# Norm of the QKV input: sums of squares spread over all partitions by two products with ones, for blocks two to eight

## Chip, cores and metric

The kernel runs on one core of a Trainium2 chip. The metric is the device time of one execution in microseconds (us). The core has five engines that work side by side and wait for each other through semaphores: TensorE (PE, with its weight loads shown as PEld), VectorE (DVE), ScalarE (ACT), GpSimd (POOL) and SyncE (SP, which here only issues DMAs).

## The reference

`x` is 2 x 2048 x 576 (batch, tokens, channels), with 16 heads of 36 channels. What bears on the change is the first RMS norm and the QKV product:

```python
def rmsnorm(x, g, d):
    n = jnp.linalg.norm(x, axis=-1, keepdims=True)
    return x / jnp.maximum(n, EPS) * d ** 0.5 * g          # EPS = 1e-12
mod = silu(c) @ ada_w.T + ada_b                             # six parts: shift, scale, gate, twice
h = rmsnorm(x, g1, D) * (1.0 + scale_msa) + shift_msa
qkv = h @ qkv_w.T + qkv_b                                   # 576 -> 1728
q = rmsnorm(q, qg, HEAD_DIM);  k = rmsnorm(k, kg, HEAD_DIM) # per head
# then attention, projection, gated residual, a second norm, a gelu MLP of 2304, gated residual
```

All of it is in float32. The kernel feeds TensorE with values split into a high and a low part (type fp32r), so that three products stand for one.

## The kernel before

The program has a QKV stage (up to about 437 us of the span) and a main stage (attention, projection, MLP). The change lies in the QKV stage alone.

**Tiling.** Channels lie on partitions: 576 are four chunks of 128 and one of 64 (`KC` = 5 chunks). Tokens are cut into eight blocks of 512 (`BLK`), numbered i = 0 to 7, alternating between the two batch rows (r = i % 2). Each block has four tiles of 128 tokens (`TPB` = 4, t = 0 to 3). Only the first iteration and the last (of `NIT` = 4, two blocks each) are written out; those between are a hardware loop with the same body.

**One tile on TensorE** (`tile`, L787 on). The 1728 output columns stand in four PSUM banks of 432 columns, in two halves h = 0, 1. One half is 28 products of 128x432 (L798). A half may start when VectorE has emptied the same banks of the tile before. After the second half come nine transposes of the q and k of the tile before (`turn`, L753), which must wait for VectorE's `scale` (L597) of that tile. TensorE executes in order, so whatever stands behind a waiting transpose waits too.

**One tile on VectorE** (`body`, L681 on), in this order: `evac` of half 0 (L612 and L614, adding the bias); `scale` of the tile before (L590, L592, L594, L597); `evac` of half 1; the sums over heads of the squares that ScalarE has made meanwhile (L703, behind ACT L444); two, one or no `dot` products for the later modulation (L659); the low part of the transposed tile before (L603).

**The norm of the next block** runs beside the tiles of the current one. POOL sums the squared chunks into `sq_hi` and `sq_lo` (128 partitions x 512 tokens); the sum over the partitions is left. In tile t = 1, after half 0, TensorE runs `sum_squares`: for each group of 128 tokens two products with the squares as weights and two columns of ones moving (L737, L738), so that the sums stand one token to a partition, as 128x8, in `RT`. VectorE bounds them from below (L392, right after `evac` half 0), ScalarE takes the root (L366), VectorE the reciprocal (L397, right after `scale`, ahead of `evac` half 1), and after half 1 TensorE's `spread_norm` (L745, four float32 products of 128x128, each shown as two instructions) brings the result back to all partitions as 128x512 in PSUM, `RB`. At t = 2, ahead of `evac` half 0, VectorE multiplies the whole block with it (L406, 128x2560, reading `RB`); ScalarE applies the modulation (L369) and makes the high part (L386), POOL the low one.

Block 0's norm is made in the same way before the first tile, and keeps its form.

Of the kernel before, what the change touches and what calls it, by code (L numbers as in the profile page):

```python
# [10 lines left out]
ACT = mybir.ActivationFunctionType  # L11
ALU = mybir.AluOpType
AX = mybir.AxisListType

P = 128
# [5 lines left out]
KC = KF + 1  # L21
DP = KC * P
BLK = 512
# [13 lines left out]
EPS = 1e-12  # L37
# [7 lines left out]
def wait(eng, sem, value):  # L45

    if isinstance(value, int) and value <= 0:
        return
    eng.wait_ge(sem, value)
# [108 lines left out]
def qkv_phase(nc, ctx, sb, ps, first_unit, xT, cT, ada, adan, adab, wqkv, qkvb, pb, f1b, f2b, gains, qk_hi, qk_lo, v_s, m_s,  # L158
# [5 lines left out]
    st = ctx  # L164

    def sem(name):
        return ctx.enter_context(nc.semaphore("a_" + name))

    xb = sb(st, "xb", [P, 2, KC, BLK])
    tmp = sb(st, "tmp", [P, KC, BLK])  # L170
# [16 lines left out]
    rs = sb(st, "rs", [P, TPB, 2])  # L187
    sq_hi = sb(st, "sq_hi", [P, BLK], F32R)
    sq_lo = sb(st, "sq_lo", [P, BLK], F32R)
# [3 lines left out]
    w_raw2 = sb(st, "w_raw2", [P, KC, PIECE])  # L193
    w_raw3 = sb(st, "w_raw3", [P, KC, PIECE])
    root_gain = sb(st, "root_gain", [P, 1])

    awp = aw[:, 1].rearrange("p (k c) -> p k c", k=KC)
    aws, awn = (aw[:, j, 0:KC * D].rearrange("p (m c) -> p m c", m=KC) for j in range(2))
# [23 lines left out]
    sq_done, sqsum, sqhi_done, sqlo_done = sem("sq_done"), sem("sqsum"), sem("sqhi_done"), sem("sqlo_done")  # L222
    ss_done, nrm_done, rb_mm = sem("ss_done"), sem("nrm_done"), sem("rb_mm")
    r_max, r_done, xr_done = sem("r_max"), sem("r_done"), sem("xr_done")
# [11 lines left out]
    RB, MOD1 = ps[:, 4, :], ps[:, 5, 0:KC * B].rearrange("p (m b) -> p m b", b=B)  # L236
# [127 lines left out]
    def norm_act(act, i):  # L364
        act.wait_ge(r_max, i + 1)
        act.activation(rs[:], rs[:], ACT.Sqrt).then_inc(nrm_done, 1)  # L366

    def affine(act, r, m):
        act.activation(tmp[:, m], tmp[:, m], ACT.Identity, bias=mod[:, SHIFT_MSA, m, r:r + 1],  # L369
                       scale=mod[:, SCALE_MSA, m, r:r + 1]).then_inc(aff_done, 1)  # L370

    def prep_act(act, i, r, part):

        if part == 0:
            act.wait_ge(x_ld[r], 16 * (i // B + 1) if isinstance(i, int) else 8 * (i - r) + 16)
            act.wait_ge(hlo_done, KC * i)
            act.activation(tmp[:], xb[:, r], ACT.Square).then_inc(sq_done, 1)
        elif part == 1:
            norm_act(act, i)
        elif part == 2:  # L380
            act.wait_ge(xr_done, i + 1)
            for m in range(KC):
                affine(act, r, m)
            act.wait_ge(aff_done, KC * (i + 1))
            wait(act, qkv_mm, 2 * TPB * (i - 1))
            act.activation(h_hi[:, r], tmp[:], ACT.Copy).then_inc(hhi_done, 1)  # L386

    def bounded(dve, i):

        dve.wait_ge(ss_done, i + 1)  # L390
        wait(dve, rb_mm, i)
        dve.tensor_scalar(rs[:], RT, EPS * EPS, None, ALU.max).then_inc(r_max, 1)  # L392

    def reciprocal(dve, i):

        dve.wait_ge(nrm_done, i + 1)
        dve.reciprocal(rs[:], rs[:]).then_inc(r_done, 1)  # L397

    def prep_dve(dve, i, r, part):
        if part == 0:  # L400
            bounded(dve, i)
        elif part == 1:
            reciprocal(dve, i)
        else:
            dve.wait_ge(rb_mm, i + 1)
            dve.tensor_tensor(tmp[:], xb[:, r], RB.unsqueeze(1).to_broadcast([P, KC, BLK]),  # L406
                              ALU.mult).then_inc(xr_done, 1)

    HQ = slice(0, H), slice(H, QKG)

# [80 lines left out]
    def dve_part(dve):  # L491
# [22 lines left out]
        def w_low(q, half, done):  # L514

            dve.wait_ge(whi_done, q + 1)
            ks, cols = W_HALVES[half], slice(q * PIECE, (q + 1) * PIECE)
            dve.tensor_tensor(w_lo[:, ks, cols], raw[q][:, ks], f32(w_hi[:, ks, cols]), ALU.subtract).then_inc(done, 1)
# [38 lines left out]
        dve.wait_ge(mod_done, 1)  # L557
        dve.tensor_scalar(mod[:, SCALE_MSA], mod[:, SCALE_MSA], root_gain[:, 0:1], None, ALU.mult).then_inc(mod_done, 1)
        w_low(0, 0, wlo_done)
        bounded(dve, 0)  # L560
        reciprocal(dve, 0)
        w_low(0, 1, wlo_done)
        dve.wait_ge(mod_done, 2)
        dve.wait_ge(modn_add, 1)
# [113 lines left out]
        def body(it, first, last):  # L678
            for r in range(B):
                i = B * it + r  # L680
                more = not (last and r == 1)  # L681
                for t in range(TPB):
                    tt, early = TPB * i + t, first and r == 0 and t < 2
                    if last and r == 1 and t == TPB - 1:
                        last_half(0)
                        scale(tt - 1, t + 1)
                        last_scale(0)
                        turned_low(tt - 1)
                        last_half(1)
                        last_scale(1)  # L690
                        continue
                    if more and t == 2:
                        prep_dve(dve, i + 1, 1 - r, 2)
                    evac(tt, i, t, 0, early)
                    if more and t == 1:
                        prep_dve(dve, i + 1, 1 - r, 0)
                    if not (first and r == 0 and t == 0):
                        scale(tt - 1, t + 1)
                    if more and t == 1:
                        prep_dve(dve, i + 1, 1 - r, 1)  # L700
                    evac(tt, i, t, 1, early)
                    dve.wait_ge(sqt_done, tt + 1)
                    dve.tensor_reduce(ssb[:], sqb.rearrange("p (g d) -> p g d", d=HD), AX.X,  # L703
                                      ALU.add).then_inc(red_done, 1)
                    if first and r == 0 and t == 0:
                        for m in range(2, KC):
                            shift(1, m, prod)
                    for m in (DOTS_FIRST if first and r == 0 else DOTS if more else DOTS_LAST)[t]:
                        dot(it, i, r, m)
                    if not (first and r == 0 and t == 0):  # L710
                        turned_low(tt - 1)
# [10 lines left out]
    def pe_part(pe):  # L722
# [5 lines left out]
                               start=k == 0, stop=k == KC - 1)  # L728
            return mm

        def sum_squares(i):

            pe.wait_ge(sqlo_done, i + 1)
            wait(pe, xr_done, i)
            for t in range(TPB):
                cols = slice(t * P, (t + 1) * P)
                pe.matmul(RT[:, t], sq_hi[:, cols], ones[:, 0:2], start=True, stop=False)  # L737
                mm = pe.matmul(RT[:, t], sq_lo[:, cols], ones[:, 0:2], start=False, stop=True)  # L738
            mm.then_inc(ss_done, 1)

        def spread_norm(i):

            pe.wait_ge(r_done, i + 1)
            for t in range(TPB):
                mm = pe.matmul(RB[:, t * P:(t + 1) * P], rs[:, t, 0:1].to_broadcast([P, P]), ident[:], start=True, stop=True)  # L745
            mm.then_inc(rb_mm, 1)

        def turn(tt, t, chunks=range(QKC)):

# [25 lines left out]
            mm = modulate(m)  # L775
        mm.then_inc(mod_mm, 1)
        pe.wait_ge(ones_done, 2)
        sum_squares(0)
        spread_norm(0)

        def tile(i, r, t, first, last):
            tt = TPB * i + t
            cols = slice(t * P, (t + 1) * P)
            final = last and r == 1 and t == TPB - 1
            for h in range(2):
                if not (first and r == 0 and t == 0):
                    pe.wait_ge(evac_done, 2 * tt + h - 1)  # L787
                for k in range(KC):
                    if first and r == 0 and t == 0:
                        if h == 0:  # L790
                            pe.wait_ge(hlo_done, k + 1)
                        if k == 0:
                            pe.wait_ge((wlo_done, wlo_last)[h], 3 - h)
                        if k == W_HALVES[1].start:
                            pe.wait_ge((wlo_done, wlo_last)[h], 4)
                    for n, (w, a) in enumerate(passes(k, w_hi, w_lo, h_hi, h_lo)):
                        for q in (2 * h, 2 * h + 1):
                            mm = pe.matmul(ps[:, q, 0:PIECE], a[:, r, k, cols], w[:, k, q * PIECE:(q + 1) * PIECE],  # L798
                                           start=k == 0 and n == 0, stop=k == KF and n == 1)
                    if final and h == 1 and k == KF - 2:  # L800
                        turn(tt - 1, t + 1)
                mm.then_inc(qkv_mm, 1)
                if t == 1 and h == 0 and not (last and r == 1):
                    sum_squares(i + 1)
                if t == 1 and h == 1 and not (last and r == 1):
                    spread_norm(i + 1)
            if not (final or first and r == 0 and t == 0):
                turn(tt - 1, t + 1)

# [1051 lines left out]
```

## Time and profile before

| | |
|---|---|
| median of three runs | 2885.67 us (2885.53 to 2886.21) |
| the profiled execution | 2886.55 us, span 2884.8 us |
| granted TensorE clock, mean | 0.998 |
| PE busy | 2858.4 us, 99% of the span |
| DVE busy | 1971.2 us, 68% |
| ACT busy | 1574.2 us, 55% |
| POOL busy | 215.5 us, 7% |

Times in the rows are microseconds from the start of the span unless marked ns. A timeline row gives start, duration, engine, line, operation, what is written and read, and in square brackets the idle time of the engine before it with what ended it. TensorE's instructions overlap, so their durations say less than the distance from one start to the next.

### The profile page before, as it was taken

Reading aid. Unit: us, or ns where it says so; the run is one execution under the profiler, and the core shown is the slowest. Engines: PE = TensorE matmul, PEld = TensorE weight load, DVE = VectorE, ACT = ScalarE, POOL = GpSimd, SP = SyncE. Lnnn points to the kernel's source line nnn. Section 1 sums busy time; section 2 is a strip of 40 time slices with the busy share of each in tenths; the row PEclk is TensorE's granted clock in tenths of the full one; section 3 lists DMA queues with packets and bytes.
Section 4 is the critical chain, followed back from the end, with each engine's and each line's share of the span. In section 5 each row is a group of like instructions: output and inputs, shape, how many; then the busy total and the mean of one; then the engine's idle time right before and its main releaser. Section 6 shows DMA issues by size and latency. Waiting matters only on the chain.

```text
span 2884.8 us, 35304 instructions
## 1 busy us (share of the span) xinstructions
PE 2858.4 (99%) x12990; PEld 2172.0 (75%) x12990; DVE 1971.2 (68%) x2727; ACT 1574.2 (55%) x1924; POOL 215.5 (7%) x163
## 2 busy tenths in 40 slices
PE   8999999999999999999999999999999999999999
PEld 7999995666666666666666666788888888888887
DVE  7777677899898889888989987844344243424342
ACT  4334326777677677677677676634344343434342
POOL 1322310101000000000000000090000000000000
PEclk9999999999999999999999999999999999999999
DMA  6455554322222222222222223432222222322121
GB/s 231 158 190 177 181 162 141 89 74 64 82 81 78 79 83 64 78 84 79 75 79 71 75 84 94 132 127 87 75 87 74 82 79 87 98 91 87 41 69 50
DMA packets 238454, 282.67 MB, mean 98 GB/s; under 512 B 34960, under 2 KB 144016, under 8 KB 237392
## 3 DMA queue, kind: packets, MB, share of 16 engines
q1 hardware_dynamic: 233408, 270.80, 30.5%
q10 hardware_dynamic: 4880, 9.70, 1.0%
q8 instruction: 99, 1.62, 0.2%
q14 instruction: 67, 0.55, 0.1%
HBM read 195.50 MB, written 84.67 MB: 97 GB/s over the span
## 4 chain that ended last, share of the span: by engine, by line
PE 94%; DVE 3%; ACT 1%; DMA 1%; issue 1%; SPq 0%; POOL 0%; POOLq 0%; DVEq 0%; ACTq 0%
PE ps L1651 16%; PE ps L1676 16%; PE ps L1721 15%; PE ps L1739 15%; PE ps L1663 14%; PE ps L798 12%; PE ps L1697 4%; PE ps L1662 2%; PE ps L753 1%; ACT gated L1320 1%; DMA gain<-kg 0%; DVE p_lo L1463 0%; DVE x L1523 0%; PE ps L745 0%; DVE w_lo L1516 0%
## 5 line engine op out<-in xcount | busy, mean ns | idle before, releaser
L1264 ACT ACTIVATE p_r<-ps 128x1024 f32<-128x1024 f32 x512 | 494.2, 1067 | 397.5 <-PE ps L1651 397.5
L1463 DVE TENSOR_TENSOR p_lo<-p_r,p_hi 128x1024 fp32r<-128x1024 f32 x512 | 613.5, 1219 | 0.0
L1651 PE MATMUL ps<-qT,kT 128*128 128x512 f32 x2048 | 570.2, 395 | 3.4 <-DMA kT<-qk_hi_scratch 2.3
L1264 ACT ACTIVATE prob<-ps 128x1024 f32<-128x1024 f32 x512 | 484.0, 1056 | 3.6 <-PE ps L1651 3.6
L1651 PEld LDWEIGHTS ps<-qT,kT 128*128 128x128 f32 x2048 | 381.0, 189 | 133.9 <-issue 51.4
L1662 PE MATMUL ps<-prob,vp 128*64 128x512 f32 x1024 | 453.1, 595 | 0.0
L1663 PE MATMUL ps<-prob,vp 128*37 128x512 f32 x1024 | 451.7, 594 | 0.0
L1593 DVE TENSOR_TENSOR a_lo<-act,a_hi 128x512 fp32r<-128x512 f32 x144 | 101.4, 704 | 502.1 <-ACT a_hi L1307 502.1
L1457 DVE CAST p_hi<-p_r 128x1024 fp32r<-128x1024 f32 x512 | 350.2, 694 | 128.5 <-ACT p_r L1264 124.2
L1739 PE MATMUL ps<-a_hi,w 128*128 128x512 f32 x1296 | 410.8, 389 | 0.0
L1676 PE MATMUL ps<-p_hi,vx 128*128 128x512 f32 x1024 | 399.3, 390 | 0.6 <-issue 0.2
L1676 PE MATMUL ps<-p_lo,vx 128*128 128x512 f32 x1024 | 398.4, 389 | 0.0
L1305 ACT ACTIVATE act<-ps,f1b_t 128x512 f32<-128x512 f32 x144 | 99.3, 690 | 499.9 <-PE ps L1721 498.4
L1663 PEld LDWEIGHTS ps<-prob,vp 128*37 128x37 f32 x1024 | 111.5, 114 | 247.6 <-issue 247.6
L1721 PE MATMUL ps<-mh_hi,w_hi 128*128 128x512 f32 x720 | 281.0, 390 | 2.6 <-DVE w_lo L1516 2.6
L1739 PEld LDWEIGHTS ps<-a_hi,w 128*128 128x128 f32 x1296 | 243.3, 188 | 50.9
L1721 PE MATMUL ps<-mh_hi,w_lo 128*128 128x512 f32 x720 | 280.2, 389 | 0.0
L1739 PE MATMUL ps<-a_lo,w 128*128 128x512 f32 x720 | 280.2, 389 | 0.0
L1676 PEld LDWEIGHTS ps<-p_hi,vx 128*128 128x128 f32 x1024 | 192.2, 188 | 43.4 <-issue 2.1
L1721 PE MATMUL ps<-mh_lo,w_hi 128*128 128x512 f32 x576 | 224.1, 389 | 0.0
L1676 PEld LDWEIGHTS ps<-p_lo,vx 128*128 128x128 f32 x1024 | 192.3, 188 | 40.1
L798 PE MATMUL ps<-w_hi,h_hi 128*128 128x432 f32 x640 | 182.0, 365 | 3.5 <-DVE h_lo L530 3.5
(195 smaller groups left out, 3561.9 us busy)
## 6 DMA issues: line engine op xcount, KB each, us to landing
w_raw<-w SPq DMA_DIRECT2D x144, 320.0 KB, 2.9
qk_hi_scratch<-aw SPq DMA_DIRECT2D x32, 576.0 KB, 3.2
qk_lo_scratch<-aw SPq DMA_DIRECT2D x32, 576.0 KB, 4.4
kT<-qk_hi_scratch SPq DMA_DIRECT2D x128, 144.0 KB
qT<-qk_hi_scratch SPq DMA_DIRECT2D x128, 144.0 KB
v_scratch<-stv SPq DMA_DIRECT2D x32, 512.0 KB, 2.6
vp<-v_scratch SPq DMA_DIRECT2D x16, 1024.0 KB, 8.9
xb<-xT SPq DMA_DIRECT2D x8, 1280.0 KB, 10.8
```

The source lines that it names most:

```text
L798: mm = pe.matmul(ps[:, q, 0:PIECE], a[:, r, k, cols], w[:, k, q * PIECE:(q + 1) * PIECE], start=k == 0 and n == 0, stop=k == KF and n == 1)
L1264: act.activation(out, ps[:, 2 * slot:2 * slot + 2, :].rearrange("p a b -> p (a b)"), ACT.Exp).then_inc(exp_done, 1)
L1457: dve.tensor_copy(p_hi[:, q % HIGHS], p_r[:, j]).then_inc(phi_done, 1)
L1463: dve.tensor_tensor(p_lo[:, j], p_r[:, j], f32(p_hi[:, q % HIGHS]), ALU.subtract).then_inc(plo_done, 1)
L1593: dve.tensor_tensor(a_lo[:, slot], act32[:, slot], f32(a_hi[:, slot]), ALU.subtract).then_inc(alo_done, 1)
L1651: mm = pe.matmul(ps[:, 2 * (entry % RING) + h, :], kT[r][:, h, kt * P:(kt + 1) * P], qT[:, u % 2, h], start=True, stop=True)
L1662: pe.matmul(OA[0:64], vp[r][:, kt, 0:64], prob[:, j, 0:BLK], start=False, stop=False)
L1663: pe.matmul(OBK[64:VW], vp[r][:, kt, 64:VW], prob[:, j, BLK:2 * BLK], start=False, stop=False).then_inc(fv_mm, 1)
L1676: mm = pe.matmul(out, vx[r][:, j, h], part[:, h * BLK:(h + 1) * BLK], start=j == 0 and n == 0, stop=j == NS - 1 and n == 1)
L1697: mm = pe.matmul(proj_bank(i, m), w[:, k, m * P:(m + 1) * P], a[:, k], start=k == 0 and n == 0, stop=k == KF and n == len(parts) - 1)
L1721: mm = pe.matmul(ps[:, 5 + slot, :], w[:, slot, c], a[:, i % 2, c], start=c == 0 and n == 0, stop=c == KF and n == 1)
L1739: mm = pe.matmul(ps[:, m, :], w, a[:, slot], start=k == 0 and n == 0, stop=k == FC - 1 and n == len(parts) - 1)
```

## The change

For the norms of blocks 1 to 7 (seven times) the sum over partitions is made by two products with the 128x128 ones as weights and the 512 columns of `sq_hi`, then `sq_lo`, moving. So the sums stand on all partitions at once, in `RB` (PSUM). ScalarE takes the root of the 512 columns out of PSUM into a new SBUF tile `rb`. VectorE then bounds `rb` from below and takes its reciprocal, both over 512 columns, at the place where it took the reciprocal of 8 columns before. The four products of `spread_norm` and the bound over 8 columns go. The multiplication of the block reads `rb` in SBUF in place of `RB` in PSUM. Block 0 keeps the old form.

```diff
+    rb = sb(st, "rb", [P, BLK])
@@ prep_act, part 1
-            norm_act(act, i)
+            act.wait_ge(ss_done, i + 1)
+            act.activation(rb[:], RB, ACT.Sqrt).then_inc(nrm_done, 1)
@@ VectorE
-    def prep_dve(dve, i, r, part):
-        if part == 0:
-            bounded(dve, i)
-        elif part == 1:
-            reciprocal(dve, i)
-        else:
-            dve.wait_ge(rb_mm, i + 1)
-            dve.tensor_tensor(tmp[:], xb[:, r], RB.unsqueeze(1).to_broadcast([P, KC, BLK]),
-                              ALU.mult).then_inc(xr_done, 1)
+    def invert_norm(dve, i):
+        dve.wait_ge(nrm_done, i + 1)
+        dve.tensor_scalar(rb[:], rb[:], EPS, None, ALU.max).then_inc(r_max, 1)
+        dve.wait_ge(r_max, i + 1)
+        dve.reciprocal(rb[:], rb[:]).then_inc(r_done, 1)
+
+    def apply_norm(dve, i, r):
+        dve.wait_ge(r_done, i + 1)
+        dve.tensor_tensor(tmp[:], xb[:, r], rb[:].unsqueeze(1).to_broadcast([P, KC, BLK]),
+                          ALU.mult).then_inc(xr_done, 1)
@@ VectorE, body
                     if more and t == 2:
-                        prep_dve(dve, i + 1, 1 - r, 2)
+                        apply_norm(dve, i + 1, 1 - r)
                     evac(tt, i, t, 0, early)
-                    if more and t == 1:
-                        prep_dve(dve, i + 1, 1 - r, 0)
                     if not (first and r == 0 and t == 0):
                         scale(tt - 1, t + 1)
                     if more and t == 1:
-                        prep_dve(dve, i + 1, 1 - r, 1)
+                        invert_norm(dve, i + 1)
                     evac(tt, i, t, 1, early)
@@ TensorE (the old functions stay for block 0 as sum_first and spread_first)
+        def sum_squares(i):
+            pe.wait_ge(sqlo_done, i + 1)
+            pe.wait_ge(xr_done, i)
+            pe.matmul(RB, ones[:], sq_hi[:], start=True, stop=False)
+            pe.matmul(RB, ones[:], sq_lo[:], start=False, stop=True).then_inc(ss_done, 1)
@@ TensorE, tile
                 if t == 1 and h == 0 and not (last and r == 1):
                     sum_squares(i + 1)
-                if t == 1 and h == 1 and not (last and r == 1):
-                    spread_norm(i + 1)
```

## Rows read from the trace of the kernel before

**Rows 1.** The page: busy time of each engine over the span.
```profile
PE 2858.4 (99%) x12990; PEld 2172.0 (75%) x12990; DVE 1971.2 (68%) x2727; ACT 1574.2 (55%) x1924; POOL 215.5 (7%) x163
```

**Rows 2.** Chain in order of time (start, us, what): tile 1 of block 1.
```profile
96.47 5.52 PE ps L798 x28
...
102.78 5.61 PE ps L798 x28
108.39 0.89 PE ps L745 x8
```

**Rows 3.** Timeline of VectorE, tiles 1 and 2 of block 1.
```profile
103.07 0.16 DVE L392 TENSOR_SCALAR rs<-ps 128x8 f32<-128x8 f32 x1
103.14 0.17 DVE L590 TENSOR_SCALAR rt<-rt 128x32 f32<-128x32 f32 x1
...
105.28 0.20 DVE L397 RECIPROCAL rs<-rs 128x8 f32<-128x8 f32 x1
108.43 0.76 DVE L612 TENSOR_TENSOR stq<-ps,bias 128x576 f32<-128x576 f32 x1 [2.95 <-PE ps L798]
...
114.80 2.81 DVE L406 TENSOR_TENSOR tmp<-xb,ps 128x2560 f32<-128x2560 f32 x1
...
119.42 1.36 DVE L597 TENSOR_TENSOR stq<-stq,rt 128x1152 f32<-128x1152 f32 x1
```

**Rows 4.** Timeline at the same transpose: free (120.92) and kept waiting (428.07).
```profile
120.92 1.10 PEld L753 LDWEIGHTS ps<-ident,stq 128*128 128x128 f32 x9
122.01 0.64 PE L798 MATMUL ps<-w_hi,h_hi 128*128 128x432 f32 x2
...
426.66 1.36 DVE L597 TENSOR_TENSOR stq<-stq,rt 128x1152 f32<-128x1152 f32 x1
...
428.07 0.97 PEld L753 LDWEIGHTS ps<-ident,stq 128*128 128x128 f32 x9 [0.18 <-DVE stq L597]
429.03 0.64 PE L798 MATMUL ps<-w_hi,h_hi 128*128 128x432 f32 x2
```

**Rows 5.** Timeline of VectorE, tile 1 of blocks 0, 2, 4 and 6.
```profile
56.84 0.20 DVE L397 RECIPROCAL rs<-rs 128x8 f32<-128x8 f32 x1
58.59 0.76 DVE L612 TENSOR_TENSOR stq<-ps,bias 128x576 f32<-128x576 f32 x1 [1.56 <-PE ps L798]
...
156.37 0.20 DVE L397 RECIPROCAL rs<-rs 128x8 f32<-128x8 f32 x1
158.21 0.76 DVE L612 TENSOR_TENSOR stq<-ps,bias 128x576 f32<-128x576 f32 x1 [1.64 <-PE ps L798]
...
256.18 0.20 DVE L397 RECIPROCAL rs<-rs 128x8 f32<-128x8 f32 x1
257.79 0.76 DVE L612 TENSOR_TENSOR stq<-ps,bias 128x576 f32<-128x576 f32 x1 [1.41 <-PE ps L798]
...
356.28 0.20 DVE L397 RECIPROCAL rs<-rs 128x8 f32<-128x8 f32 x1
357.36 0.76 DVE L612 TENSOR_TENSOR stq<-ps,bias 128x576 f32<-128x576 f32 x1 [0.88 <-PE ps L798]
```

**Rows 6.** Timeline of VectorE, the norm of one block in the main stage.
```profile
1853.90 0.42 DVE L1498 TENSOR_SCALAR rb<-rb 128x512 f32<-128x512 f32 x1
1854.36 3.36 DVE L1500 RECIPROCAL rb<-rb 128x256 f32<-128x256 f32 x2
1857.76 0.49 DVE L1503 TENSOR_SCALAR rb<-rb,gain 128x512 f32<-128x512 f32 x1
```

**Rows 7.** Groups by line and shape (busy, mean ns of one | idle before).
```profile
L592 DVE RECIPROCAL rt<-rt 128x32 f32<-128x32 f32 x31 | 10.9, 353 | 1.1
...
L1283 ACT ACTIVATE rb<-ps 128x512 f32<-128x512 f32 x1 | 0.6, 599 | 4.5 <-PE ps L1710 4.5
```

**Rows 8.** TensorE at the stage's end: window (length, busy, clock, DMA), then timeline.
```profile
434.00:435.00 1.00, 0.00 (x0) 0.52 1.01 360
...
435.60 1.33 PE L761 MATMUL ps<-ident,stq 128*128 128x128 f32 x5 [2.98 <-DVE stq L649]
```

More of the change, by code:

```diff
@@ L386, in prep_act, with bounded, reciprocal @@
             act.activation(h_hi[:, r], tmp[:], ACT.Copy).then_inc(hhi_done, 1)
-    def bounded(dve, i):
-        dve.wait_ge(ss_done, i + 1)
-        wait(dve, rb_mm, i)
+    def bounded(dve):
+        dve.wait_ge(ss_done, 1)
         dve.tensor_scalar(rs[:], RT, EPS * EPS, None, ALU.max).then_inc(r_max, 1)
-    def reciprocal(dve, i):
+    def reciprocal(dve):
+        dve.wait_ge(nrm_done, 1)
+        dve.reciprocal(rs[:], rs[:]).then_inc(r_done, 1)
+    def invert_norm(dve, i):
         dve.wait_ge(nrm_done, i + 1)
-        dve.reciprocal(rs[:], rs[:]).then_inc(r_done, 1)
-    def prep_dve(dve, i, r, part):
-        if part == 0:
-            bounded(dve, i)
-        elif part == 1:
-            reciprocal(dve, i)
-        else:
-            dve.wait_ge(rb_mm, i + 1)
-            dve.tensor_tensor(tmp[:], xb[:, r], RB.unsqueeze(1).to_broadcast([P, KC, BLK]),
-                              ALU.mult).then_inc(xr_done, 1)
+        dve.tensor_scalar(rb[:], rb[:], EPS, None, ALU.max).then_inc(r_max, 1)
[5 more added lines that the diff above has]
+                          ALU.mult).then_inc(xr_done, 1)
     HQ = slice(0, H), slice(H, QKG)
@@ L559, in dve_part @@
         w_low(0, 0, wlo_done)
-        bounded(dve, 0)
-        reciprocal(dve, 0)
+        bounded(dve)
+        reciprocal(dve)
         w_low(0, 1, wlo_done)
@@ L729, in modulate, with sum_first @@
             return mm
-        def sum_squares(i):
-            pe.wait_ge(sqlo_done, i + 1)
-            wait(pe, xr_done, i)
+        def sum_first():
+            pe.wait_ge(sqlo_done, 1)
             for t in range(TPB):
@@ L739, in sum_squares, with spread_first @@
             mm.then_inc(ss_done, 1)
-        def spread_norm(i):
-            pe.wait_ge(r_done, i + 1)
+        def spread_first():
+            pe.wait_ge(r_done, 1)
             for t in range(TPB):
@@ L777, in pe_part @@
         pe.wait_ge(ones_done, 2)
-        sum_squares(0)
-        spread_norm(0)
+        sum_first()
+        spread_first()
         def tile(i, r, t, first, last):
```

## The prediction

> **What bounds the kernel now.** I read the busy table first: TensorE is at work for 99% of the span, VectorE for 68% [rows 1]. So work taken off TensorE looks like time won, and work put on VectorE looks hidden. Both hold only if no wait stands close behind, so the next view is the chain in order of time through the QKV stage: it is TensorE's L798, L753, L745 almost without a break, and tile 1 of each block has two extra pieces, the sums between its halves and the spread after them [rows 2]. Then I read VectorE's timeline at the same place, for the one thing that TensorE takes from it there: the transposes (L753) behind tile t = 2 wait for `scale` (L597) in that tile. In block 1 this L597 runs from 119.42 to 120.78 [rows 3], and the first weight load of the transposes starts at 120.92 [rows 4]. TensorE thus reaches the transposes only just after VectorE has finished for it. In the middle of a block this margin, and not the 68%, is what VectorE has to spare.
>
> **How large the margin is.** Free, the next L798 starts at 122.01, that is 1.23 after L597's end at 120.78. Kept waiting, as at 428.07, it starts at 429.03, and L597 had ended at 426.66 + 1.36 = 428.02: 1.01 after it [rows 4]. VectorE can be 1.23 - 1.01 = 0.22 us later there at today's pace of TensorE; any more moves L798, and all of the engine's order behind it, by the excess. The other blocks show the same distance (scale's end to weight load 0.14 in each of the seven).
>
> **What leaves and comes on TensorE.** Between the first half's end (96.47 + 5.52 = 101.99) and the second half's start (102.78) lie 0.79 us for the eight small products; the spread takes 0.89 [rows 2]. The second half takes 5.61 against 5.52 for the first; I leave half of this 0.09 out of the account. Two products of 512 columns come: 28 of 432 columns take 5.52, or 0.197 each, so 0.234 for 512 columns and 0.47 for two. TensorE's own saving is 0.79 - 0.47 = 0.32 ahead of the second half and 0.89 after it, about 1.25 per block with the rest, 8.8 over seven. But this is not a term of the sum. TensorE would come to the transposes of tile 2 1.25 earlier, and they wait for L597. What counts is when L597 ends.
>
> **What VectorE does in its place.** The bound over 8 columns delays L590 by 0.07 (103.07 to 103.14 [rows 3]); it goes, so L590 to L597 come 0.07 earlier. The reciprocal of 8 columns at the end of `scale` (105.28) also goes. In its slot start the bound and the reciprocal of 512 columns. The main stage has both: bound to reciprocal 0.46, and two reciprocals of 256 columns in 3.36, or 1.68 each [rows 6]. Against 353 ns for 32 columns [rows 7] this is (1.72 - 0.353) / 224 = 6.1 ns per column, with 1.72 for one alone of the pair (their overlap is 0.08); 512 in one instruction come to 1.72 + 256 x 0.0061 = 3.29. At most it is the whole 3.36. The next instruction starts 0.08 before the end, as after L597 (120.78 would be its end, and in block 1 the small reciprocal starts at 105.28 for an L597 that starts at 104.01 and lasts 1.36). So `evac` of the second half can start at the old start of L397 - 0.07 + 0.46 + 3.21 = L397 + 3.60.
>
> It stood behind TensorE and not behind VectorE before, so only a part of the 3.60 shows. In block 1 it started at 108.43, 3.15 after L397 [rows 3]; blocks 3 and 5 are alike. Delay 3.60 - 3.15 = 0.45, three times. In blocks 0, 2, 4, 6 VectorE comes late into the tile and the gap is 1.75, 1.84, 1.61 and 1.08 [rows 5]: delays 1.85, 1.76, 1.99 and 2.52. Together 9.47 us.
>
> **What of this reaches TensorE.** From `evac` of half 1 (108.43) to L406 (114.80) and L597 (119.42) [rows 3], VectorE waits only once, for ScalarE's squares, which start when that same `evac` ends; nothing in between can take up the delay. The whole 9.47 arrives at L597, seven margins of 0.22 (1.54) come off, and 7.9 us are left. TensorE's stalls at L753 are then, with the 1.25 by which it is early, delay + 1.03: 2.9, 1.5, 2.8, 1.5, 3.0, 1.5, 3.6, some 16.7 us. After tile 2 the engines fall back into step: VectorE waited there for TensorE again, so the delay of one block is neither carried into the next nor won back.
>
> **What is hidden.** The root over 512 columns: 0.60 [rows 7] in place of 0.21, on ScalarE, which may start at 101.99 + 0.47 and must be done when `scale` is, at 105.3; over 2 us of cover. In blocks 2, 4 and 6 ScalarE is late by a transfer (its copy of the transposes ends about when the sums do), still over 2 us ahead of `scale`'s end. If that cover were gone, each 0.1 would cost 0.1 per block. The multiplication reads `rb` from SBUF: 2.81 for 2560 columns is 1.10 ns per column, L597's 1.36 for 1152 from SBUF alone is 1.18 [rows 3]; by that rate it would be 3.02, 0.21 more. The difference of the two rows gives 1.45 / 1408 = 1.03 per column with a fixed part, the line on which both lie. I take nothing, with ends -0.1 and +0.2 per block (-0.7 to +1.5 in all). SP's loads and stores are released by the same instructions as before and move with them. POOL has finished its sums before the products and starts again behind ScalarE's high part, which is 16 us ahead of its need.
>
> On the reciprocal the Trainium skill speaks, in "VectorE: DVE Perf Modes", section "First, the fixed hardware budget": it is an iterative divide with a repeat count of eight. Read as eight cycles per column at the page's 0.96 GHz this is an estimate of 4.27 us for 512 columns; the delays would each be 0.98 larger and the loss 14.8 us. The main stage's rows give 6.1 ns per column, not 8.3, and the rows decide. The rule does point the right way: a reciprocal is far from the one column per cycle of other operations.
>
> **Sum.** The profiled execution took 2886.55, 1.75 more than its span; with 7.9 it is 2894.5. It stood 0.88 above the median, so the changed kernel's median is 2885.67 + 7.9 = 2893.6.
>
> **Rivals.**
> *The clock falls in the stalls.* At the end of the stage TensorE stood still but for four transposes from 431.2, and the granted clock went to its lower level (1.2 of 2.4 GHz) at about 434.5 [rows 8]. The stalls of blocks 0, 2, 4, 6, with about 1 us of transposes behind them, leave L798 silent for 3.8 to 4.6 us, as long as that. For it: the length. Against it: the even blocks alone reach it, and dense products surround them. At half the clock a product of 432 columns takes 0.36 in place of 0.197; some 3.5 us at that level lose 1.6. One or two falls, or one in each late block at the most: +1.6 to +6.4, typically 2896.8. The Trainium skill, "TensorE: Matmul & The Clock Gate", section "HAM oscillation — how this bites in real kernels", describes such falls from waits between bursts; by that rule it would be this case, and the trace agrees on the fall at 434.5.
>
> *The late blocks don't add.* If the delay above 0.45 in blocks 0, 2, 4 and 6 were taken up by something that I count as rigid (in 2, 4, 6 VectorE's lateness comes from a transfer, which might land earlier relative to the engines once the stage is longer), each block would lose 0.45 - 0.22 = 0.23, in all 1.6: 2887.3. For it: 6.3 of the 7.9 come from these four. Against it: the transfer is issued by VectorE's and TensorE's progress, so it moves along.
>
> *The added work is hidden, and TensorE's saving shows: the other side.* If bound and reciprocal fit into VectorE's idle time ahead of `evac` half 1, VectorE would be led by TensorE, 0.32 earlier, and would win 0.22 + 0.32 = 0.54 per block: -3.8, 2881.9. It decides where bound and reciprocal together, with their handover, stay under 3.15 - 0.32 + 0.07 = 2.90 in the odd blocks and under 0.83 in block 6. The rows' 3.67 exceeds all of these. Even so TensorE's 8.8 could not come through, since L597 holds the transposes. It would take another error, a larger margin at L753, to win more.
>
> **How the numbers follow.** Forecast 0.71, with its own range 2892.5 to 2896.5 (multiplication -0.7 to +1.5, reciprocal up to +0.5, a slower restart of a TensorE that stood longer up to +0.7). Clock 0.11, late blocks not adding 0.13, hidden 0.05. Range 2889 to 2897.5: it leaves out most of the last two and the far end of the clock. 0.2% is 5.8 us, about what a measurement of this kernel tells from no change. Slower: 0.69 of the forecast and 0.11, so 0.80. Within: 0.13, 0.02 of the forecast's low end, 0.02 of the hidden case, so 0.17. Faster: 0.03, from a hidden case with a larger margin.
>
> **What the changed profile would show.** Eight instructions of the float32 spread in place of 64. A reciprocal of 128x512 at 3.3 us seven times. TensorE waiting for L597 at L753 seven times, 16.7 us together, 1.5 in odd and 2.8 to 3.6 in even blocks. No idle time ahead of `evac` half 1 in tile 1. The stage's end 7.9 us later, and the main stage unchanged. I am wrong if L753's waits are small, if the late blocks' waits are like the others', or if the reciprocal is under 2.5 us.

## The result

The changed kernel takes 2897.67 us (median of seven, 2896.05 to 2899.95) against 2886.21 for the kernel before on the same chip: 11.5 us slower, ratio 1.0040, 95% interval 1.0031 to 1.0050. The forecast was slower by 7.9 us (2893.6, range 2889 to 2897.5). The direction was right, and so was the wait that was named for it. The size was 3.6 us too small and the time lies just outside the range: the fall of TensorE's clock, which the forecast had left out of its sum, came on top. The profiled execution took 2897.67 us too.

The page of the changed kernel, its span and busy times:

```profile
span 2895.9 us, 35101 instructions
PE 2857.0 (99%) x12892; PEld 2166.1 (75%) x12892; DVE 1992.3 (69%) x2727; ACT 1576.7 (54%) x1924; POOL 214.8 (7%) x163
```

TensorE did 1.4 us less [rows 1], VectorE 21 us more, and the span grew by 11.1. Neither busy time tells of a loss on TensorE; its order does. VectorE's timeline of the changed kernel in tiles 1 and 2 of block 1 answers to [rows 3]:

```profile
105.31 1.36 DVE L601 TENSOR_TENSOR stq<-stq,rt 128x1152 f32<-128x1152 f32 x1
106.58 0.42 DVE L403 TENSOR_SCALAR rb<-rb 128x512 f32<-128x512 f32 x1
107.04 3.35 DVE L405 RECIPROCAL rb<-rb 128x512 f32<-128x512 f32 x1
110.31 0.69 DVE L616 TENSOR_TENSOR stq<-ps,bias 128x576 f32<-128x576 f32 x1
...
116.61 2.81 DVE L410 TENSOR_TENSOR tmp<-xb,rb 128x2560 f32<-128x2560 f32 x1
...
121.24 1.36 DVE L601 TENSOR_TENSOR stq<-stq,rt 128x1152 f32<-128x1152 f32 x1
```

The bound and the reciprocal start where the small reciprocal stood; `evac` half 1 (110.31) follows without a wait, and from there on all distances are the old ones: 6.30 to L410 (before 6.37), 4.63 to L601 (before 4.62). Then TensorE's timelines of the changed kernel at the transposes of tile 2, in blocks 0 and 1, and with the products behind them in block 2, then in blocks 4 and 6:

```profile
72.60 1.20 PE L761 MATMUL ps<-ident,stq 128*128 128x128 f32 x9 [2.67 <-DVE stq L601]
...
122.65 1.20 PE L761 MATMUL ps<-ident,stq 128*128 128x128 f32 x9 [1.30 <-DVE stq L601]
123.61 0.64 PE L806 MATMUL ps<-w_hi,h_hi 128*128 128x432 f32 x2
...
173.87 2.08 PE L761 MATMUL ps<-ident,stq 128*128 128x128 f32 x9 [2.51 <-DVE stq L601]
175.59 1.07 PE L806 MATMUL ps<-w_hi,h_hi 128*128 128x432 f32 x2
176.46 0.92 PE L806 MATMUL ps<-w_lo,h_hi 128*128 128x432 f32 x2
177.18 0.68 PE L806 MATMUL ps<-w_hi,h_lo 128*128 128x432 f32 x2
177.70 0.56 PE L806 MATMUL ps<-w_hi,h_hi 128*128 128x432 f32 x2
...
277.28 2.18 PE L761 MATMUL ps<-ident,stq 128*128 128x128 f32 x9 [3.05 <-DVE stq L601]
...
380.83 1.20 PE L761 MATMUL ps<-ident,stq 128*128 128x128 f32 x9 [2.06 <-DVE stq L601]
```

All of them wait for `scale`. In block 1 the transposes and products behind go at their usual pace (0.96 from the first transpose to the next product). In block 2 they don't: 1.72 for the same transposes, and products 0.36 apart in place of 0.197 (176.46 to 177.18 is two of them). One-microsecond windows of TensorE there (length, busy, granted clock, DMA share, GB/s) say why:

```profile
173.00:174.00 1.00, 0.14 (x1) 1.00 0.00 0
174.00:175.00 1.00, 1.00 (x6) 0.51 0.00 0
...
177.00:178.00 1.00, 1.00 (x6) 0.78 0.10 37
```

From 174.0 on the granted clock is at its lower level (1.2 of 2.4 GHz) for 3.4 us. It is so also from 276.4 to 283.3 (block 4, 6.8 us, begun inside the wait) and from 382.2 to 385.7 (block 6, 3.4 us, begun 0.4 us after the products had started again). In block 0 it stays at its upper level, though TensorE waited 2.67 there, longer than in blocks 2 and 6. The waits of TensorE at the transposes of tile 2, in all:

```profile
PE ps L761 <- DVE stq L601: 14.2, 7, 3.1
```

The start of the first product behind the delayed transposes (L798 before, L806 after) in blocks 0 to 6 shows where the time goes. The third column is how much later it is, the fourth by how much this grew in the block:

| block | before | after | later | grown | forecast |
|---|---|---|---|---|---|
| 0 | 72.18 | 73.56 | 1.38 | 1.38 | 1.63 |
| 1 | 122.01 | 123.61 | 1.60 | 0.22 | 0.23 |
| 2 | 171.80 | 175.59 | 3.79 | 2.19 | 1.54 |
| 3 | 221.59 | 226.44 | 4.85 | 1.06 | 0.23 |
| 4 | 271.37 | 279.11 | 7.74 | 2.89 | 1.77 |
| 5 | 321.16 | 330.99 | 9.83 | 2.09 | 0.23 |
| 6 | 370.95 | 381.79 | 10.84 | 1.01 | 2.30 |
| last transposes | 435.60 | 447.96 | 12.36 | 1.52 | 0 |

Blocks 0 and 1, before the clock first falls, match; in block 0 the match is closer still, since the stage's first product started 0.20 us earlier in this trace (31.07 against 31.27), so that 1.58 were lost there. The growth that the forecast lacks stands in blocks 2 to 5 and after 6, each time around a stretch at the lower clock; block 6 itself grew by 1.3 less than forecast. Of the 12.36 us the main stage gives 1.3 back; its wait for the first K transfer shrinks by more, from 2.3 to 0.3 us.

### The profile page after: what moved, and what is told of

Read it like the earlier page. It is cut to its first block, busy times and chain, and to the rows that moved or that the text cites. A ratio compares the mean times of both kernels' runs of the same rounds, so it can differ in the third digit from the quotient of the medians.

```text
span 2895.9 us, 35101 instructions
## 1 busy us (share of the span) xinstructions
PE 2857.0 (99%) x12892; PEld 2166.1 (75%) x12892; DVE 1992.3 (69%) x2727; ACT 1576.7 (54%) x1924; POOL 214.8 (7%) x163
## 4 chain that ended last, share of the span: by engine, by line
PE 87%; DVE 7%; issue 2%; DMA 2%; ACT 2%; SPq 0%; POOL 0%; POOLq 0%; DVEq 0%; ACTq 0%
PE ps L1657 16%; PE ps L1682 16%; PE ps L1727 15%; PE ps L1745 15%; PE ps L1669 14%; PE ps L806 6%; PE ps L1703 4%; PE ps L1668 2%; DMA qk_lo_scratch<-aw 1%; DVE stq L601 1%; PE ps L761 1%; DVE tmp L410 1%; ACT gated L1326 1%; DVE stq L616 1%; DMA gain<-kg 0%
## 5 line engine op out<-in xcount | busy, mean ns | idle before, releaser
L806 PE MATMUL ps<-w_hi,h_hi 128*128 128x432 f32 x640 | 183.0, 367 | 3.7 <-DVE h_lo L534 3.5
```

## Experiments

Each was timed against the kernel before on the same chip; its medians were 2886.24, 2886.41 and 2886.53 us in the three groups (four kernels each).

### Without the long reciprocal

```diff
-        dve.tensor_scalar(rb[:], rb[:], EPS, None, ALU.max)
-        dve.reciprocal(rb[:], rb[:])
+        dve.tensor_scalar(rb[:, 0:8], rb[:, 0:8], EPS, None, ALU.max)
+        dve.reciprocal(rb[:, 0:8], rb[:, 0:8])
```

> The changed kernel with bound and reciprocal over 8 of the 512 columns (504 columns of rb stay roots, so the norm is left out for them). Theory (VectorE's 512-column work ahead of evac half 1 makes scale late, and scale gates the transposes of tile 2): no delay, no stall over 0.8 us at L761, clock never falls; VectorE's order starts 0.32 us earlier and the margin of 0.22 is used up: 0.54 per block, 3.8 us under before, 2882.4. Rival (TensorE's saved products are time won as soon as VectorE is not slowed): 8.8 under before, 2877.4. Rival (the loss comes from the new products or the root, not from the reciprocal): about as the changed kernel, 2897.7.

Measured 2881.55 us, ratio 0.9983 (0.9974 to 0.9992): 4.7 under before, against 3.8 by the theory and 8.8 by the first rival. The kernel is faster than before with the new products and the root in it; the 512 columns on VectorE cost it all. TensorE's waits, although VectorE is no longer slowed:

```profile
PE ps L761 <- DVE stq L601: 3.2, 7, 0.5
```

Each of the seven transposes of tile 2 still waits 0.45 for `scale`: the margin was too small even for TensorE's own saving.

### VectorE's work alone, TensorE as before

```diff
                         prep_dve(dve, i + 1, 1 - r, 1)
+                        dve.tensor_scalar(rb[:], c_b[:, 0, 0:BLK], EPS, None, ALU.max).then_inc(silu_step, 1)
+                        dve.wait_ge(silu_step, 2 * i + 5)
+                        dve.reciprocal(rb[:, 0:472], rb[:, 0:472]).then_inc(silu_step, 1)
```

> The kernel before with only VectorE's work added in the same place: a bound over 512 and a reciprocal over 472 columns of other data, together as long as the new slot. TensorE keeps its old products and arrives 1.25 us later at the transposes of tile 2. Theory: L597 ends as late as in the changed kernel, so the pure waits cost the same, 6.5 to 7.9 us; but TensorE's stalls are 1.25 shorter each (at most about 2.3 us), too short for the clock to fall: 2893 to 2894. Rival (the clock's falls do not hang on the length of the stall, or the whole 11.5 us is pure waiting): 2897.7.

Measured 2892.67 us, ratio 1.0022 (1.0013 to 1.0031): 6.4 over before. `scale` ends at 122.70 in block 1 (changed kernel 122.60), so TensorE is held up to the same time; it arrives later, waits at most 1.5 us in the trace, and the clock stays at its upper level up to the stage's end, whose last transposes start at 442.27, 6.7 later than before. That TensorE's saving doesn't enter the sum is borne out. With it, the stall only gets longer. And 6.4 is what the waiting costs with no fall of the clock; the changed kernel's 11.5 needs something beside it.

### The changed kernel with filler on TensorE in the stall

```diff
+            if t == 2 and not (last and r == 1):
+                pe.wait_ge(nrm_done, i + 2)
+                for _ in range(6):
+                    pe.matmul(RB[:, 0:PIECE], ones[:], w_hi[:, 0, 0:PIECE], start=True, stop=True)
             if not (final or first and r == 0 and t == 0):
                 turn(tt - 1, t + 1)
```

> The changed kernel with six products of 432 columns without use on TensorE ahead of the transposes in tile 2 of blocks 0 to 6, about 1.2 us of work inside stalls of 1.5 to 3 us. Theory (falls of the clock after the long stalls cost what waiting alone doesn't explain): the stalls' free part is as short as before, the clock stays at its upper level until the stage's end, about 6 us less than the changed kernel: 2891 to 2892. Rival (no clock effect, only waiting): 2897.7, unchanged, since the filler stands in time that is lost anyway.

Measured 2894.58 us, ratio 1.0030 (1.0018 to 1.0041): 3.1 less than the changed kernel (each against its own run of before: +8.3 in place of +11.5). TensorE's timeline in block 2, and its last transposes:

```profile
171.30 1.33 PE L816 MATMUL ps<-w_hi,ones 128*128 128x432 f32 x6
173.99 1.20 PE L761 MATMUL ps<-ident,stq 128*128 128x128 f32 x9 [1.36 <-DVE stq L601]
174.94 0.64 PE L806 MATMUL ps<-w_hi,h_hi 128*128 128x432 f32 x2
...
442.90 1.33 PE L769 MATMUL ps<-ident,stq 128*128 128x128 f32 x5 [2.99 <-DVE stq L653]
```

The transposes of block 2 start within 0.12 us of the changed kernel's, but take 0.95 and not 1.72, and no window between 50 and 440 us shows a granted clock under 1. The stage ends at 442.90, 7.30 after before and 5.06 ahead of the changed kernel: this is the price of the clock. Only 3.1 of it reach the end: the main stage's first wait for K is now 3.2 us, and 0.3 in the changed kernel, which is more than the difference. So the expectation was right on the stage and 3 us too low on the total.

That the clock fell in the other executions of the changed kernel too is seen from their mean granted clocks. They stand in two groups, 0.990 to 0.991 and 0.995 to 0.996; those of the kernel before stand at 0.992 to 0.994 and 0.997 to 0.999, and those of the filler run at 0.994 and 0.997 to 0.998. 0.002 of 2896 us at half the clock are an estimated 12 us more at the lower level.

### The multiplication of the block behind `scale`

```diff
 (ACT)  t = 2: tile(i, t) ahead of prep_act(act, i + 1, 1 - r, 2)
 (DVE)
-                    if more and t == 2:
-                        apply_norm(dve, i + 1, 1 - r)
                     evac(tt, i, t, 0, early)
                     ...
+                    if more and t == 2:
+                        apply_norm(dve, i + 1, 1 - r)
                     evac(tt, i, t, 1, early)
```

> The changed kernel with the multiplication of the block (L410, 2.81 us) moved on VectorE from ahead of evac half 0 to behind scale in tile 2, and ScalarE's tile work of t = 2 put ahead of its modulation. Theory (only the order ahead of scale in tile 2 binds): scale ends 2.8 us earlier, no stall in odd blocks and at most some tenths in late ones, TensorE's saving shows: 8 to 9 us under before, 2877.5 to 2878.5. Rival (the wait moves to the next transposes, of tile 3, since evac half 1 and ScalarE's work are now later): about 1 to 3 us per block lost there, 2885 to 2895.

Measured 2923.44 us, ratio 1.0131 (1.0116 to 1.0147): a miss of 45 us, by neither of my mechanisms. No transposes wait, but the first product of each next block does:

```profile
PE ps L808 <- POOL h_hi L70: 33.7, 7, 5.7
```

The multiplication feeds ScalarE's modulation and then POOL, and their chain had less to spare than I had put down. Before, POOL's last low part in block 1 ends at 129.8 and block 2's first product starts at 134.0, so the slack is 4.2 us. ScalarE's modulation started 8.5 us after the transposes of tile 1 (117.64 against 109.11) and now starts 17.2 after them (130.84 against 113.65), 8.7 later. The stalls before a block also pull the clock down (44 us at the lower level in all, 13.7 before, the latter at the start of the main stage).

### The dot products of tile 1 in tile 2

```diff
-        DOTS = ((0, 1), (2, 3), (), (4,))
-        DOTS_FIRST = ((), (0, 1), (), (2, 3, 4))
+        DOTS = ((0, 1), (), (2, 3), (4,))
+        DOTS_FIRST = ((), (), (0, 1), (2, 3, 4))
```

> The changed kernel with the two dot products of tile 1 (L663, 1.5 us together) moved to tile 2 on VectorE, behind scale. Theory (what stands on VectorE between evac half 1 of tile 1 and scale in tile 2 sets the end): the margin at L761 grows by 1.5 us. No stall in odd blocks, some tenths to 1.8 us in blocks 0, 2, 4, 6, the clock stays up: about 2.5 us under the kernel before, 2883 to 2885. Rival (the wait moves to the transposes of tile 3, or the dots cost as much there): 2890 or more.

> As e6_dots_later, and the reciprocal in two halves of 256 columns, one ahead of evac half 1 and one behind it, where VectorE waits 1.23 us for ScalarE's squares. Theory: 1.2 us of the reciprocal then stand in time that is idle anyway; stalls of 0.1 to 0.9 us in blocks 0, 2, 4, 6 alone, most of TensorE's 8.8 us shows: 2879 to 2880, faster than both kernels by 0.2%. Rival (the second half delays the reduction and so the root for scale, and the wait moves on by as much): as e6_dots_later or slower, 2884.

> The kernel before with the same move of the dot products and nothing else. Control: before the change TensorE's own order bounds the stage, so room on VectorE is worth nothing: 2886.2, no change. Rival (the dots were already in the way): up to 3 us faster.

> The changed kernel with bound and reciprocal over 8 columns (norm left out for the other 504) and the dot products moved. Theory: the 3.2 us of waits at L761 that were left with the short reciprocal go, and TensorE's full saving shows: 8.8 under before, 2877.4. Rival (the saving was mis-sized or the engines catch on something else): as with the short reciprocal alone, 2881.6.

The diff is the move alone, which all four have. Measured, in the order above: the changed kernel with the move 2900.66 us (ratio 1.0054, interval 1.0040 to 1.0068), with the split reciprocal beside it 2893.81 (1.0023, 1.0013 to 1.0032), the kernel before with the move 2891.58 (1.0020, 1.0011 to 1.0029), and the changed kernel with the short reciprocal and the move 2888.58 (1.0008, 0.9999 to 1.0017). All four theories missed; the rival of the first (the wait moves to tile 3, 2890 or more) came true. The control is the telling one: with no other edit than the move, the kernel before loses 5.2 us. VectorE's timeline of the control in tile 2 of block 1, then POOL's:

```profile
125.21 2.63 DVE L659 CUSTOM_DVE_ANT_0 w_raw<-aw,c_b 128x576 f32<-128x576 f32 x1
...
127.88 1.73 DVE L659 CUSTOM_DVE_ANT_0 w_raw<-aw,c_b 128x576 f32<-128x576 f32 x1
```

```profile
122.59 4.63 POOL L351 TENSOR_TENSOR h_lo<-tmp,h_hi 128x2048 fp32r<-128x2048 f32 x1 [22.53 <-ACT h_hi L386]
127.30 1.69 POOL L70 TENSOR_TENSOR h_hi<-tmp,h_hi 64x512 fp32r<-64x512 f32 x1
```

The same dot product takes 0.75 in tile 1 (112.05 in the trace of before). Beside POOL's passes over `tmp` and `h_hi` it takes 2.63 and 1.73. It isn't slowed there, it is held: the first ends at 127.84, 0.62 after the first pass (122.59 + 4.63 = 127.22), the second at 129.61, 0.62 after the second pass (128.99), and so in all seven blocks. In the changed kernel with the move the first dot begins earlier beside the same pass and takes 3.02; it ends 0.61 after the pass all the same. So 1.5 us of work became 4.4, and the transposes of tile 3 waited 0.57 to 0.64 each (in the changed kernel with the move 2.2 to 2.3). On the margin in tile 2 they say only that its waits shrank: in the changed kernel with the dots moved, the transposes of tile 2 wait not at all in the odd blocks and at most 0.8 us in the others.

### `scale` first in tile 2

```diff
+                    if more and t == 2:
+                        scale(tt - 1, t + 1)
                     evac(tt, i, t, 0, early)
-                    if not (first and r == 0 and t == 0):
+                    if not (first and r == 0 and t == 0 or more and t == 2):
                         scale(tt - 1, t + 1)
```

`evac` of half 0 takes 1.1 us, and TensorE needs it only after the transposes, for which it needs `scale`. The swap puts nothing beside POOL's work.

> The changed kernel with scale put ahead of evac half 0 on VectorE in tile 2 alone. Theory (the wait at L761 is set by when scale ends in tile 2): scale ends 1.1 us earlier, each of the seven waits is 1.1 us shorter, none is over 2.2 us and the clock stays at its upper level: -1.3 against the kernel before, 2885, so 12 us less than the changed kernel. Rival (evac half 0, now later, holds up TensorE's tile 3 instead): 2890 or more.

Measured 2886.30 us, ratio 1.0000 (0.9991 to 1.0009): the whole loss is gone by the order of two steps. The clock stays at its upper level up to the stage's last wait, though one wait is 2.3 us. The waits at the transposes:

```profile
PE ps L763 <- DVE stq L601: 7.4, 7, 2.3
```

> The changed kernel with bound and reciprocal over 8 columns (norm left out for the other 504) and scale first in tile 2. Theory: the 3.2 us of waits at L761 that the short reciprocal alone left go to zero and TensorE's full saving of 1.25 per block shows: 8.8 under before, 2877.5. Rival (the saving was mis-sized): as with the short reciprocal alone, 2881.6.

Measured 2876.74 us, ratio 0.9969 (0.9957 to 0.9981): 9.8 under before. No transposes of tile 2 wait. This is TensorE's full saving, put at 8.8; the small reciprocal alone had shown 4.7. The trace has it at 1.31 us in each of blocks 1 to 6, against 1.25 in the prediction, so 9.2 over seven; the rest of the 9.8 isn't told apart from the start of the stage, whose first product comes at 30.5 to 32.0 us from trace to trace, whatever the kernel.

```diff
         dve.wait_ge(r_max, i + 1)
-        dve.reciprocal(rb[:], rb[:]).then_inc(r_done, 1)
+        dve.reciprocal(rb[:, 0:BLK // 2], rb[:, 0:BLK // 2]).then_inc(r_done, 1)
@@ behind evac half 1 of tile 1
+                        dve.reciprocal(rb[:, BLK // 2:BLK], rb[:, BLK // 2:BLK]).then_inc(r_done, 1)
```

> The changed kernel with scale first in tile 2 and the reciprocal in two halves of 256 columns, one ahead of evac half 1 and one behind it, where VectorE waits for ScalarE. Nothing is placed beside POOL's work. Theory: waits of 0 in odd and 0.3 to 0.9 us in blocks 0, 2 and 4: 7.2 under before, 2879, by 0.25% faster than the kernel before. Rival (the second half costs its full 1.7 us in the chain): 2885.

Measured 2878.79 us, ratio 0.9974 (0.9964 to 0.9984): 7.7 under before, 7.2 expected. VectorE in tile 1 of block 1:

```profile
104.65 1.75 DVE L405 RECIPROCAL rb<-rb 128x256 f32<-128x256 f32 x1
106.99 0.76 DVE L616 TENSOR_TENSOR stq<-ps,bias 128x576 f32<-128x576 f32 x1 [0.58 <-PE ps L810]
...
108.03 1.74 DVE L707 RECIPROCAL rb<-rb 128x256 f32<-128x256 f32 x1
109.68 1.30 DVE L709 TENSOR_REDUCE ssb<-w_raw 128x32 f32<-128x1152 f32 x1
```

The first half fits ahead of TensorE's second half with 0.58 to spare; the second stands where VectorE waited 1.23 for ScalarE's squares. What is left of the waits:

```profile
PE ps L765 <- DVE stq L601: 1.3, 3, 0.7
```

> As e13_scale_first_split, and in blocks 2, 4 and 6 the two dot products of tile 1 moved to tile 3, behind POOL's work on h_lo (in tile 2 they had taken 2.6 and 1.7 us in place of 0.76). Theory: no waits left but 0.3 us in block 0: 2878. Rival (dots in tile 3 delay scale for the next block's first transposes): 2880 or more, slower than e13_scale_first_split.

Measured 2877.81 us, ratio 0.9970 (0.9958 to 0.9981): 8.7 under before. The last waits are gone. This version leaves nothing out and is faster than both kernels, as the one without the moved dots is. It lies 1 us under that one; the intervals of the two ratios overlap, and in the traces the stage's last transposes start 1.3 us earlier (427.47 against 428.74), as much as the waits that are gone.

## Why the prediction was right and where it was wrong

*The margin at L753.* "1.23 - 1.01 = 0.22 us" held. With a delay forecast as 0.45 in blocks 1, 3 and 5, the cost in block 1 was 0.22 (forecast 0.23), and in the filler run 0.26, 0.24 and 0.23. The short reciprocal showed it from the other side: 0.45 of waiting left with no delay at all.

*VectorE's slot.* Put at 3.67 from the bound to the next instruction, it measured 3.73 (106.58 to 110.31); the reciprocal 3.35 in place of 3.29. The multiplication out of SBUF took 2.81, as out of PSUM, so "I take nothing" held. The root over 512 columns stayed hidden. TensorE's waits that follow from the slot were forecast at 16.7 us together and are 14.2 in the trace; 1.5 of the 2.5 between them are block 6.

*The late blocks.* The term of the sum was 9.47 - 1.54 = 7.9 us; the stage with the clock held up measured 7.30. It splits into 1.41, 1.47, 1.91 and 1.78 for blocks 0, 2, 4, 6 (forecast 1.63, 1.54, 1.77, 2.30) and 0.73 for the odd ones. Block 6 is the mis-sized one: its lateness hangs on the landing of a store, and ScalarE's wait for that was 3.8 us before and 2.5 in the changed kernel, where block 6 grew by only 1.0. The rival that these delays would not add was right for a part of one block and wrong for the rest.

*The clock.* This is the step that failed. The prediction had the trigger, the places and the price, and then put the fall at nothing in its sum and gave it 0.11 as a rival, on the ground that "the even blocks alone reach it, and dense products surround them". The dense surroundings did not help: in the profiled run it fell in three of those four blocks, for 3.4, 6.8 and 3.4 us, and cost 5.06 us at the stage's end by the filler run. The prediction's own price, about 1.6 us for each 3.5 us, agrees: 13.7 us at the lower level make 6.3, and block 6, 0.8 less late than with the filler, took some of it back. With these 5.06, the 7.30 of waiting and the 1.3 that the main stage takes back, the kernel before's 2885.67 becomes 2896.8; another 0.5 is its own median, which is 2886.21 in the seven runs.

The row that this rival was compared with was also misread. The prediction has the fall "at about 434.5" after TensorE had stood still from 431.2. The window from 434 to 435 in [rows 8] has 0.52, nearly all of it at the lower level, so the clock fell at 434.0, after 2.8 us with four transposes in them, and not after 3.3. The stalls of the even blocks were forecast at 2.8 to 3.6 us, so all four were as long as that, and the fall belonged into the likeliest case.

What decides where it falls stays open. The wait's length alone doesn't: in the changed kernel it fell at waits of 2.06, 2.51 and 3.05 us and not at 2.67; with the dots moved and the reciprocal split it fell at 1.85, and with `scale` first it did not at 2.29. So that the shorter stalls of VectorE's work alone (at most 1.48) kept the clock up fits, but no length can be read from these runs below which it is safe.

*The main stage "unchanged".* Not quite: the wait for K at its start moved between 0.3 and 3.2 us from kernel to kernel, while 12.36 at the stage's end became 11.1, and 7.30 became 8.0. The stretch at the lower clock there moves too: 13.7 us before, 10.2 in the changed kernel. The traces show that both move; what sets them, and how they add up to the difference, was not looked into.

*The rival on the other side.* "Hidden" was priced at -3.8 and measured at -4.7 with the reciprocal cut short. That "TensorE's 8.8 could not come through, since L597 holds the transposes" was right for the order as it is, and `scale` put first in tile 2 released them: -9.8.

*A wrong statement.* The prediction puts ScalarE's high part "16 us ahead of its need". In the trace of before it ends at 123.7, 10.3 us ahead of the next block's first product; 16.4 is the distance from the start of ScalarE's modulation (117.64). POOL, which works behind it, ends 4.2 us ahead. Nothing in the sum rested on it, but the late multiplication was built on it and failed for it.

## What to carry to other kernels

Before moving work from the engine that is busy 99% of the time to one that is busy 68%, look at the nearest wait of the first on the second and measure its margin; here it was 0.22 us against 3.7 us of new work. If the chain on the second engine is the one that gates, order it by who needs what first: swapping two steps, and cutting one long instruction so that its halves fill two idle gaps, turned 11.5 us of loss into 7.7 of gain. And a stall on TensorE of 2 to 3 us can cost more than its own length: here three of four such stalls brought the clock down. Where VectorE has room, look also at what POOL does there at that time.

## What the runs showed of the hardware

A dot product on VectorE with both inputs in SBUF took 0.75 us alone and 2.63 and 1.73 where it met POOL's passes, since it was held until the pass had ended, and ended 0.62 after it. The Trainium skill, "GPSIMD Engine Reference", section "Specifications", says that the two engines share their SBUF interfaces and contend when VectorE's instruction runs in a two-port mode or has two SBUF inputs; the control's trace agrees, and shows that the price can be larger than the work itself. A small instruction is held too. In the kernel before, `scale` in tile 3 of block 1 meets POOL's second pass (POOL's timeline, then VectorE's):

```profile
128.50 1.29 POOL L70 TENSOR_TENSOR h_hi<-tmp,h_hi 64x512 fp32r<-64x512 f32 x1
128.84 0.99 DVE L590 TENSOR_SCALAR rt<-rt 128x32 f32<-128x32 f32 x1
```

The bound over 32 columns, with one input, takes 0.17 elsewhere and here ends at 129.83, 0.04 after POOL. Whether it runs in the two-port mode, the traces don't show. Not held in the same traces, with as long a time beside POOL as alone: `evac` (0.76 and 0.45) and the low part of the transposes (1.35), which read one input from PSUM, the sum over heads (1.35) and the reciprocal of 32 columns (0.35).

On the reciprocal, 512 columns took 3.35 us (6.5 ns each with the fixed part) and two of 256 took 1.75 and 1.74: cutting it costs about 0.1 us.
